# First attention of a gated block: rows turned before they are normalised, the norm applied in the additions, and four engine programs reordered

## The chip, the cores and the metric

One core of one Trainium2 chip runs the whole kernel as one program. The metric is the device time of one execution in microseconds; lower is better.

## The reference

Two layers of gated cross-attention and feed-forward work on x (4 x 256 tokens of 256 features) beside a context of 4 x 256 rows of 128. LN is a layer norm without gains.

```python
# layer 0, attention: the mixing is along the features of x
q = ctx @ Wq0.T + bq ; k = ctx @ Wk0.T + bk           # [4, 256, 128]
att = softmax(q @ k.T, -1)                            # [4, 256, 256], its rows sum to 1
x = x + tanh(g_xattn[0]) * einsum('bln,bmn->blm', LN(x), att)
# layer 0, feed-forward: both products with ternary weights and rows rounded to 8 bits
x = x + tanh(g_ffn[0]) * bit_linear(silu(gate) * up, down_w)    # gate, up = bit_linear(LN(x), gate_w)
# layer 1, attention: 16 heads of 128, q and k with an rms norm
x = x + tanh(g_xattn[1]) * heads(LN(x), ctx, Wq, Wk, Wv) @ Wo
# layer 1, feed-forward: 64 experts, the best 8 of a row, and a shared one
x = x + tanh(g_ffn[1]) * moe(LN(x))
```

With r = 1 / sqrt(var + eps) and m = the mean of a row of x, the first mixing is r * (x @ att.T) - r * m, because every row of att sums to 1. A constant added to a row doesn't change its LN.

## The kernel before

The 1024 tokens are 8 row tiles of 128 (two for each of 4 batches b). Each engine has one program in which the order of the steps is written out by hand as far as the first six of 32 groups of the second attention (a group is one pair of heads of one batch, AHEAD = 6); from there a loop over g runs in the same order for all groups, and then the experts follow. Engines meet through semaphores: a step begins with the waits it needs and ends with an increment. A step that waits holds up everything behind it in its engine's program.

The steps that matter here, by engine:

- SyncE issues all loads in one fixed order: ctxT, the first attention's weights, x in two halves (l_x), the gate weights, gains, down weights, then the head weights `raw` of pairs 0 and 1 (l_hqk, line 326), and more. Its later loads wait for a step: load_vo(2) for fuse_vo(0), load_qk(2) for low_w(0).
- TensorE: query_key (L829) and energy (L844) make the scores of the first attention; turn_rows_0 (L807) turns the normalised rows u of a batch; turn_att (L852) turns its attention, mix (L862) multiplies both. turn_q1, gate_0, up_0 (L878, L885) and turn_q2, down (L904, L912) are the feed-forward, one row tile at a time. fuse_vo (L1026) multiplies value and output weights. turn_rows_1 (L815) turns the normalised rows for the second attention, proj_q and proj_k (through the helper at L310 to L312) are its first products, and scores, turn, values and output its rest. keep_busy is 8 products whose result nobody reads.
- ScalarE: copy_qk (L1472), exp_A (L1478, two instructions with a row sum), copy_rows_0 (L1465), copy_att (L1484), abs_gate and abs_down (L1645, L1652), split_w (L1488: the head weights `raw` rounded into front_hi; it waits for l_hqk), turn_gate (L1506), copy_q1 (L1500), silu_0 (L1514), whole_m (L1596), copy_rows (L1461: the turned rows into xnT_hi).
- VectorE: stats_0 and aggr_0 (L1975, L1980: mean and variance of x), max_A (L2007), inv_A and norm_A (L2011, L2016), add_A (L2025: x + tanh(g) * mix, one instruction for the two tiles of a batch), stats_1, aggr_1, times_g1 and so on for the feed-forward, low_w (L2081: what split_w rounded away), add_down (L2119), low_rows (L1994: what copy_rows rounded away; proj_q(0) waits for it), add_output (the sum of the heads of a batch added to x, in the loop).
- GpSimd: root_0 and power_0 (L476, L477, L482) make -m and r; normalise_0 (L554) makes u = (x - m) * r, one instruction for each tile; round_gate, times_gain and the small scale steps serve the feed-forward.

Of the kernel before, what the change touches and what calls it, by code (L numbers as in the profile page):

```python
# [9 lines left out]
ALU = mybir.AluOpType  # L10
# [3 lines left out]
P = 128  # L14
BATCH, SEQ, HID, CDIM = 4, 256, 256, 128
TOK = BATCH * SEQ
TILES = TOK // P
# [15 lines left out]
EARLY = 5  # L33
# [6 lines left out]
def flamingo_kernel(nc, x_tok, ctx_tok, ctxT, qk0, bias0, gains, gate_wT, down_wT, down_tail,  # L40
                    norm_g1, norm_g2, gqk, head_qk, head_vo, router_w, expert_w, shared_w,
                    shared_down, outT, w_rows):
    with ExitStack() as ctx:
# [35 lines left out]
        rstd = sb("rstd", [P, TILES])  # L79
        u = sb("u", [P, TILES, HID])  # L80
# [84 lines left out]
        g_u0, t_u0, a_x0 = sem("g_u0"), sem("t_u0"), sem("a_x0")  # L165
# [281 lines left out]
        def _(pool):  # L447
# [166 lines left out]
            low_ctxT()  # L614
            root_0(0)
            power_0(0)
            normalise_0(0)
            normalise_0(1)
            root_0(1)
            power_0(1)  # L620
            normalise_0(2)
            normalise_0(3)
            root_0(2)
            power_0(2)
            normalise_0(4)
            normalise_0(5)
            scale_gain(g1, l_g1)
            root_0(3)
            power_0(3)
            round_gate(0)  # L630
            root_1(0)
            round_gate(1)
            power_1(0)
            root_1(1)
            power_1(1)
            scale_back_1(0)
            limit_1(0)
            normalise_0(6)
            scale_back_1(1)
            scale_gain(g2, l_g2)  # L640
            normalise_0(7)
            limit_1(1)
            times_gain(0)
            root_1(2)
            power_1(2)
            times_gain(1)
            root_2(0)
            low_ctx()
            scale_back_1(2)
            power_2(0)  # L650
            limit_1(2)
            times_gain(2)
            rms_k(0)
            root_1(3)
            power_1(3)
            times_gain(3)
            scale_back_2(0)
            scale_back_1(3)
            limit_2(0)
            root_2(1)  # L660
            times_rk(0)
            power_2(1)
            times_gain(4)
            limit_1(3)
            root_3(0)
            power_3(0)
            times_gain(5)
            normalise_1(0)
            normalise_1(1)
            scale_back_2(1)  # L670
            times_gain(6)
            limit_2(1)
            root_2(2)
            times_gain(7)
            power_2(2)
            rms_k(1)
            times_rk(1)
            scale_back_2(2)
            root_2(3)
            power_2(3)  # L680
            limit_2(2)
            rms_k(2)
            times_rk(2)
            scale_back_2(3)
            rms_q(0)
            root_3(1)
            limit_2(3)
            power_3(1)
            rms_k(3)
            pool.wait_ge(t_q2, 8)  # L690
            both_w(EARLY)
            normalise_1(2)
            rms_q(1)
            normalise_1(3)
            times_rk(3)
            low_w(EARLY + 1, 0)
            normalise_att(0, 0)
            normalise_att(0, 1)
            rms_q(2)
            root_3(2)  # L700
            power_3(2)
            normalise_att(1, 0)
            rms_k(4)
            normalise_att(1, 1)
            normalise_1(4)
            normalise_1(5)
            times_rk(4)
            rms_q(3)
            root_3(3)
            low_w(6, 1)  # L710
            low_w(EARLY + 1, 2)
            power_3(3)
            normalise_1(6)
            normalise_1(7)
            normalise_att(2, 0)
            normalise_att(2, 1)
# [2038 lines left out]
```

## Time and profile before

| | us |
|---|---|
| median of 3 runs (615.14 to 615.51) | 615.18 |
| the profiled execution | 616.09 |
| its span, first to last instruction | 614.3 |
| busy: TensorE / weight load | 603.3 / 522.6 |
| busy: VectorE / ScalarE / GpSimd | 477.9 / 422.7 / 236.7 |

TensorE's mean granted clock was 1.000 of full speed. Times inside the span are read from its start. The profiled execution is 0.9 us above the median and 1.8 us longer than its own span.

### The profile page before, as it was taken

What the parts mean: (1) busy time and instruction counts of PE and PEld (TensorE: products, weight loads), DVE (VectorE), ACT (ScalarE), POOL (GpSimd) and SP (SyncE); (2) the same over time, 40 slices, a digit from 0 to 9 for tenths busy, and PEclk for the clock granted to TensorE, in tenths of its full rate; (3) what the DMA queues carried; (4) which work ended last, traced back from release to release, by engine and by line L of the source; (5) the groups of instructions that cost most, each with busy time, mean ns of one, the idle gap of its engine ahead of it and who ended that gap; (6) DMA issues with size and microseconds to landing.
All of it is one profiled execution on the core that took longest, in us unless ns stands there. A gap on an engine that the chain in (4) does not pass through costs nothing.

```text
span 614.3 us, 11619 instructions
## 1 busy us (share of the span) xinstructions
PE 603.3 (98%) x3644; PEld 522.6 (85%) x3644; DVE 477.9 (78%) x1139; ACT 422.7 (69%) x1082; POOL 236.7 (39%) x282
## 2 busy tenths in 40 slices
PE   8979999999999999999999999999999999999997
PEld 6757899999999999999998888888887888887886
DVE  3999988987777787688876787788777676777776
ACT  6999999888888888889897344465444444443442
POOL 5999998576665566656662020000000000000000
PEclk9999999999999999999999999999999999999999
DMA  8513202000000000000030545453856466545640
GB/s 299 196 53 102 95 11 78 2 2 2 2 2 2 1 2 2 1 2 1 11 121 3 170 147 154 129 171 96 216 156 167 116 176 175 156 154 149 195 128 34
DMA packets 33653, 56.47 MB, mean 92 GB/s; under 512 B 12800, under 2 KB 13504, under 8 KB 33600
## 3 DMA queue, kind: packets, MB, share of 16 engines
q1 hardware_dynamic: 33312, 55.82, 30.4%
q8 instruction: 26, 0.43, 0.3%
q14 instruction: 27, 0.22, 0.1%
q10 hardware_dynamic: 288, 0.00, 0.0%
HBM read 53.45 MB, written 1.31 MB: 89 GB/s over the span
## 4 chain that ended last, share of the span: by engine, by line
PE 89%; DVE 5%; ACT 4%; issue 1%; POOL 1%; DVEq 0%; ACTq 0%; POOLq 0%
PE bank L310 25%; PE bank L312 25%; PE bank L311 25%; PE bank L985 4%; PE bank L960 2%; PE bank L952 2%; DVE hs L2088 1%; PE bank L912 1%; PE bank L1026 1%; PE bank L829 1%; DVE attT_lo L2182 1%; PE bank L835 1%; ACT att L1575 1%; ACT w L1478 1%; PE bank L815 1%
## 5 line engine op out<-in xcount | busy, mean ns | idle before, releaser
L1623 ACT ACTIVATE inter_hi<-inter 128x512 fp32r<-128x512 f32 x63 | 39.8, 632 | 140.5 <-DVE inter L2287 140.5
L310 PE MATMUL bank<-xnT_hi,front_hi 128*128 128x512 f32 (+1 forms) x260 | 102.0, 392 | 0.0
L312 PE MATMUL bank<-xnT_hi,front_lo 128*128 128x512 f32 (+1 forms) x260 | 101.7, 391 | 0.0
L311 PE MATMUL bank<-xnT_lo,front_hi 128*128 128x512 f32 (+1 forms) x260 | 101.6, 391 | 0.0
L2291 DVE TENSOR_TENSOR inter_lo<-inter,inter_hi 128x512 fp32r<-128x512 f32 x63 | 43.6, 692 | 37.9 <-ACT inter_hi L1623 37.3
L1575 ACT ACTIVATE att<-bank,shift,rq 128x256 f32<-128x256 f32 x128 | 71.3, 572 | 0.0
L596 POOL TENSOR_TENSOR att<-att,rowinv 128x512 f32<-128x512 f32 x60 | 63.1, 1067 | 11.1 <-DVE rowinv L2187 11.1
L2260 DVE TENSOR_TENSOR prod<-gate_s,bank 128x512 f32<-128x512 f32 x63 | 43.3, 687 | 21.6 <-PE bank L312 19.5
L2170 DVE TENSOR_REDUCE rowmax<-bank 128x2 f32<-128x512 f32 x64 | 43.6, 686 | 20.7 <-PE bank L312 20.4
L311 PEld LDWEIGHTS bank<-xnT_lo,front_hi 128*128 128x128 f32 x260 | 48.9, 188 | 11.3
L312 PEld LDWEIGHTS bank<-xnT_hi,front_lo 128*128 128x128 f32 x260 | 48.8, 188 | 11.3
L310 PEld LDWEIGHTS bank<-xnT_hi,front_hi 128*128 128x128 f32 x260 | 48.8, 188 | 11.1
L578 POOL TENSOR_TENSOR rk<-msq,minus_half 128x4 f32<-128x4 f32 x32 | 32.6, 1020 | 66.4 <-DVE msq L2159 66.4
L310 PE MATMUL bank<-inter_hi,front_hi 128*128 128x512 f32 (+1 forms) x130 | 51.2, 394 | 0.0
L312 PE MATMUL bank<-inter_hi,front_lo 128*128 128x512 f32 (+1 forms) x130 | 51.0, 393 | 0.0
L311 PE MATMUL bank<-inter_lo,front_hi 128*128 128x512 f32 (+1 forms) x130 | 51.0, 392 | 0.0
L2287 DVE TENSOR_TENSOR inter<-prod,w_all 128x512 f32<-128x512 f32 x63 | 43.6, 692 | 3.6 <-DVE prod L2260 1.8
L2182 DVE TENSOR_TENSOR attT_lo<-bank,attT_hi 128x512 fp32r<-128x512 f32 x64 | 43.1, 685 | 3.1 <-ACT attT_hi L1564 3.1
L310 PE MATMUL bank<-m_all,o_hi 128*128 128x256 f32 x128 | 39.0, 305 | 0.2 <-DVE o_lo L2197 0.2
L1619 ACT ACTIVATE gate_s<-bank 128x512 f32<-128x512 f32 x63 | 37.0, 588 | 2.2 <-PE bank L312 2.0
L1564 ACT ACTIVATE attT_hi<-bank 128x512 fp32r<-128x512 f32 x64 | 35.5, 601 | 3.5 <-PE bank L985 3.2
L310 PE MATMUL bank<-kh,qh 128*128 128x256 f32 x128 | 36.4, 284 | 0.1
(273 smaller groups left out, 1811.7 us busy)
## 6 DMA issues: line engine op xcount, KB each, us to landing
w_all<-w_rows SPq DMA_DIRECT2D x128, 128.0 KB, 3.0
raw<-in_expert_w SPq DMA_DIRECT2D x32, 384.0 KB, 3.5
wvo_raw<-in_expert_w SPq DMA_DIRECT2D x16, 384.0 KB, 3.5
e_more<-in_expert_w SPq DMA_DIRECT2D x16, 384.0 KB, 3.6
raw<-in_head_qk SPq DMA_DIRECT2D x8, 384.0 KB, 3.1
wvo_raw<-in_head_vo SPq DMA_DIRECT2D x4, 384.0 KB, 3.8
w_keep<-in_head_vo SPq DMA_DIRECT2D x4, 384.0 KB, 3.3
gate_raw<-in_gate_wT SPq DMA_DIRECT2D x2, 704.0 KB, 9.0
```

Source lines behind the costliest of these rows:

```text
L310: pe.matmul(out, l_hi, r_hi_, start=start, stop=False, skip_group_check=True)
L311: pe.matmul(out, l_hi, r_lo_, start=False, stop=False, skip_group_check=True)
L312: return pe.matmul(out, l_lo, r_hi_, start=False, stop=stop, skip_group_check=True)
L596: pool.tensor_tensor(a, a, rowinv[:, n % 2, h, :].unsqueeze(2).broadcast_to([P, 2, SEQ]), ALU.mult).then_inc(g_att, 1)
L1575: act.activation(att[:, n % 2, h, t, :], bank4(SBK[h])[:, t, :], ACT.Exp, bias=shift[:, n % 2, h, t:t + 1], scale=rq[:, n % 4, t * 2 + h:t ...
L1619: act.activation(gate_s[:, slot, :], bank[GB][:, :], ACT.Silu).then_inc(a_silu, 1)
L1623: act.activation(inter_hi[:, slot, :], inter[:, slot, :], ACT.Copy).then_inc(a_Ihi, 1)
L2170: dve.tensor_reduce(rowmax[:, n % 2, h, :], bank4(SBK[h]), AX.X, ALU.max, negate=True).then_inc(v_max, 1)
L2182: dve.tensor_tensor(attT_lo[:, h, :, :], bank4(TBK[h]), f(attT_hi[:, h, :, :]), ALU.subtract).then_inc(v_Tlo, 1)
L2260: dve.tensor_tensor(prod[:, slot, :], gate_s[:, slot, :], bank[UB][:, :], ALU.mult).then_inc(v_mul1, 1)
L2287: dve.tensor_tensor(inter[:, slot, :], prod[:, slot, :], w_all[:, par, :], ALU.mult).then_inc(v_mul2, 1)
L2291: dve.tensor_tensor(inter_lo[:, slot, :], inter[:, slot, :], f(inter_hi[:, slot, :]), ALU.subtract).then_inc(v_Ilo, 1)
```

## The change

Three parts.

1. turn_rows_0 turns x itself, and waits for the load of x; normalise_0 is gone. power_0 makes two small tiles beside r: tg_rstd = r * tanh(g) and tg_mean = m * tg_rstd. add_A scales the product by tg_rstd of its row, in one instruction for each tile; the part -tg_mean is left out of x there and comes in with add_output of the second attention, also one instruction for each tile. Between the two x is read through LN alone.
2. root_0 no longer makes -m.
3. The written-out orders of TensorE, ScalarE, VectorE and GpSimd up to the loop, or to its end where the loop is the rest, are new, with the waits that the new neighbours need. SyncE's program is unchanged.

```diff
             def root_0(b):
                 c = slice(2 * b, 2 * b + 2)
                 pool.wait_ge(v_pw1, b + 1)
-                pool.tensor_scalar(negm[:, c], mv[:, c, 0], -1.0, 0.0, ALU.mult, ALU.add)
                 pool.tensor_scalar(vare[:, c], mv[:, c, 1], 1.0, EPS, ALU.mult, ALU.add).then_inc(g_va0, 1)
 
             def power_0(b):
                 c = slice(2 * b, 2 * b + 2)
                 pool.wait_ge(g_va0, b + 1)
-                pool.tensor_tensor(rstd[:, c], vare[:, c], minus_half[:, 0:2], ALU.pow).then_inc(g_pw1, 1)
+                link_g(pool, pool.tensor_tensor(rstd[:, c], vare[:, c], minus_half[:, 0:2], ALU.pow))
+                if b == 0:
+                    pool.wait_ge(a_tg, 1)
+                link_g(pool, pool.tensor_scalar(tg_rstd[:, c], rstd[:, c], tg[:, 0:1], 0.0, ALU.mult, ALU.add))
+                pool.tensor_tensor(tg_mean[:, c], mv[:, c, 0], tg_rstd[:, c], ALU.mult).then_inc(g_pw1, 1)
-            def normalise_0(i):
-
-                pool.wait_ge(g_pw1, i // 2 + 1)
-                pool.tensor_scalar(u[:, i, :], x[:, i, :], negm[:, i:i + 1], rstd[:, i:i + 1], ALU.add,
-                                   ALU.mult).then_inc(g_u0, 1)
...
             def turn_rows_0(b, bk):
 
-                pe.wait_ge(g_u0, 2 * b + 2)
+                pe.wait_ge(l_x[b // 2], 16)
                 for k in range(KH):
                     for t in range(2):
                         mm = pe.transpose(bank4(bk)[:, k, t * P:(t + 1) * P],
-                                          u[:, 2 * b + t, k * P:(k + 1) * P], ident[:, :])
+                                          x[:, 2 * b + t, k * P:(k + 1) * P], ident[:, :])
...
             def add_A(b, bk):
                 dve.wait_ge(t_oA, b + 1)
-                if b == 0:
-                    dve.wait_ge(a_tg, 1)
-                xb = x[:, 2 * b:2 * b + 2, :]
-                dve.scalar_tensor_tensor(xb, bank4(bk), tg[:, 0:1], xb, ALU.mult, ALU.add).then_inc(v_xA, 1)
+                dve.wait_ge(g_pw1, b + 1)
+                for t in range(2):
+                    i = 2 * b + t
+                    ins = dve.scalar_tensor_tensor(x[:, i, :], bank4(bk)[:, t, :], tg_rstd[:, i:i + 1], x[:, i, :],
+                                                   ALU.mult, ALU.add)
+                ins.then_inc(v_xA, 1)
...
             def add_output(b):
 
                 dve.wait_ge(t_Y, 16 * b + 16)
-                xb = x[:, 2 * b:2 * b + 2, :]
-                dve.tensor_tensor(xb, bank4(YBK), xb, ALU.add).then_inc(v_Y, 1)
+                for t in range(2):
+                    i = 2 * b + t
+                    ins = dve.scalar_tensor_tensor(x[:, i, :], bank4(YBK)[:, t, :], tg_mean[:, i:i + 1], x[:, i, :],
+                                                   ALU.subtract, ALU.add)
+                ins.then_inc(v_Y, 1)
```

The new orders, as far as the text speaks of them. TensorE, first the old and then the new one:

```python
# before
query_key x5; energy(0, 2); query_key(1, 2, 0); energy(1, 6); energy(2, 0); turn_rows_0(0, 1)
pe.wait_ge(a_eA, 4); turn_att(0, 6); energy(3, 3); mix(0, 1); turn_att(1, 2); turn_rows_0(1, 5)
sum_abs([0, 1], 0); turn_att(2, 4); pe.wait_ge(v_abs, 1); mix(1, 0); sum_abs([2], 5); turn_rows_0(2, 7)
fuse_vo(0, 6); pe.wait_ge(v_xA, 2); keep_busy(0, 8); turn_q1(0, 0); turn_q1(1, 7); gate_0(0); up_0(0); mix(2, 4)
# after
query_key x4; energy(0, 2); query_key x2; turn_rows_0(0, 1); energy(1, 6); energy(2, 0); energy(3, 3)
turn_rows_0(1, 5); pe.wait_ge(a_eA, 4); turn_att(0, 6); mix(0, 1); turn_att(1, 2); turn_att(2, 4)
sum_abs([0, 1], 0); turn_rows_0(2, 7); pe.wait_ge(v_abs, 1); mix(1, 0); sum_abs([2], 5)
pe.wait_ge(v_xA, 2); keep_busy(0, 8); turn_q1(0, 0); mix(2, 4); gate_0(0); turn_q1(1, 7); fuse_vo(0, 6); up_0(0)
```

ScalarE's program up to silu_0(0), as a diff:

```diff
             high_ctxT()
             copy_qk(0, 0, 0, 1)
+            gates()
             copy_qk(1, 0, 1, 7)
             copy_qk(0, 1, 2, 5)
             copy_qk(1, 1, 3, 4)
-            gates()
+            exp_A(0, 2)
             copy_qk(0, 2, 4, 3)
             copy_qk(1, 2, 5, 0)
-            exp_A(0, 2)
+            copy_rows_0(0, 1)
+            split_w(0)
             exp_A(1, 6)
-            copy_rows_0(0, 1)
             exp_A(2, 0)
             copy_att(0, 6)
             abs_gate(0)
...
             copy_att(1, 2)
             copy_rows_0(1, 5)
             abs_down()
-            split_w(0)
-            turn_gate(0)
             exp_A(3, 3)
             copy_att(2, 4)
+            copy_rows_0(2, 7)
+            turn_gate(0)
             turn_gate(1)
-            copy_rows_0(2, 7)
             copy_q1(0, 0)
             load_table(ACT.Silu)
             silu_0(0)
...
             copy_q2(2, 4)
+            act.wait_ge(t_z1, 8)
+            whole_m(3, 6)
             copy_rows(0, 0, 1)
-            whole_m(3, 6)
```

VectorE's program up to the second row tile's sums:

```python
# before
stats_0(0); aggr_0(0); stats_0(1); max_A(0, 2); max_A(1, 6); aggr_0(1); inv_A(0); max_A(2, 0); norm_A(0)
inv_A(1); stats_0(2); aggr_0(2); stats_0(3); norm_A(1); aggr_0(3); inv_A(2); max_A(3, 3); add_A(0, 1)
norm_A(2); weight_scale(0, 0, 2 * INTER * HID); inv_scale(0); stats_1(0); aggr_1(0); times_g1(0)
# after
max_A(0, 2); stats_0(0); aggr_0(0); stats_0(1); inv_A(0); norm_A(0); aggr_0(1); max_A(1, 6); max_A(2, 0)
stats_0(2); aggr_0(2); stats_0(3); max_A(3, 3); inv_A(1); norm_A(1); inv_A(2); norm_A(2); add_A(0, 1)
stats_1(0); weight_scale(0, 0, 2 * INTER * HID); aggr_1(0); inv_scale(0); aggr_0(3); times_g1(0)
```

GpSimd begins with root_0(0), power_0(0), root_0(1), low_ctxT, root_0(2), scale_gain(g1), power_0(1), power_0(2), root_1(0), power_1(0) where low_ctxT stood first and normalise_0 followed each power_0. From there to the loop neighbours change places in all four programs; the set of steps of each engine is the same but for normalise_0.

## Rows read from the trace of the kernel before

**Rows 1.** The page, busy time of each engine.
```profile
PE 603.3 (98%) x3644; PEld 522.6 (85%) x3644; DVE 477.9 (78%) x1139; ACT 422.7 (69%) x1082; POOL 236.7 (39%) x282
```

**Rows 2.** Busy time in chosen stretches; last three columns: TensorE clock, DMA share, GB/s.
```profile
24.50:53.00 28.50, 23.73 (x152) 16.13 (x153) 28.27 (x68) 28.10 (x62) 27.08 (x36) 1.00 0.21 64
55.50:105.00 49.50, 49.50 (x392) 44.99 (x390) 43.63 (x126) 48.22 (x144) 45.72 (x58) 1.00 0.24 81
105.00:115.00 10.00, 9.80 (x78) 9.32 (x77) 8.96 (x30) 8.00 (x27) 6.18 (x6) 1.00 0.01 3
17.33:56.27 38.94, 33.90 (x215) 24.11 (x214) 38.56 (x95) 38.10 (x80) 36.82 (x50) 1.00 0.28 87
```

**Rows 3.** TensorE in order of time.
```profile
13.98 0.63 PE L852 MATMUL bank<-ident,w 128*128 128x128 f32 x4 [0.96 <-DVE invA L2011]
...
15.31 1.98 PE L862 MATMUL bank<-w,xT 128*128 128x256 f32 x8
...
57.18 0.39 PE L310 MATMUL bank<-front_hi,xnT_hi 128*128 128x256 f32 x1
```

**Rows 4.** ScalarE in order of time: start us, length us; idle before it in brackets.
```profile
12.30 0.47 ACT L1478 ACTIVATE w<-bank,nmA 128x256 f32<-128x256 f32 x1
...
13.21 0.59 ACT L1465 ACTIVATE xT<-bank 128x512 f32<-128x512 f32 x1
...
20.28 0.85 ACT L1488 ACTIVATE front_hi<-raw 128x768 fp32r<-128x768 f32 x1
...
27.52 0.83 ACT L1514 ACTIVATE hs<-bank,tinyB 128x704 f32<-128x704 f32 x1
...
49.50 0.69 ACT L1596 ACTIVATE m_whole<-bank,tg 128x512 f32<-128x512 f32 x1 [0.36 <-PE bank L1026]
...
55.49 0.60 ACT L1461 ACTIVATE xnT_hi<-bank 128x512 fp32r<-128x512 f32 x1 [0.43 <-PE bank L815]
```

**Rows 5.** VectorE in order of time.
```profile
17.33 0.75 DVE L2025 SCALAR_TENSOR_TENSOR x<-bank,tg,x 128x512 f32<-128x512 f32 x1 [0.54 <-PE bank L862]
17.99 0.61 DVE L2016 TENSOR_SCALAR w<-w,invA 128x256 f32<-128x256 f32 x2
...
26.02 0.95 DVE L2081 TENSOR_TENSOR front_lo<-raw,front_hi 128x768 fp32r<-128x768 f32 x1
...
34.61 1.54 DVE L2081 TENSOR_TENSOR front_lo<-raw,front_hi 128x768 fp32r<-128x768 f32 x1
...
47.32 0.48 DVE L2119 SCALAR_TENSOR_TENSOR x<-bank,tinyB,x 128x256 f32<-128x256 f32 x1
...
56.27 0.68 DVE L1994 TENSOR_TENSOR xnT_lo<-bank,xnT_hi 128x512 fp32r<-128x512 f32 x1
```

**Rows 6.** Tiles raw (first load) and x, their landings, and the DMA stretch between.
```profile
L326 SPq DMA_DIRECT2D raw<-in_head_qk x1: 576/576/576, 5.7 to 5.7; - x1
DMA to landing us min/median/max: 10.6/10.6/10.6
...
L319 SPq DMA_DIRECT2D x<-in_x_tok x2: 432/432/432, 1.6 to 2.1; - x2
...
  DMA x<-in_x_tok: 8.1, 1
...
DMA to landing us min/median/max: 6.4/6.8/7.2
...
5.70:16.30 10.60, 9.64 (x41) 7.07 (x40) 6.91 (x27) 8.26 (x23) 7.92 (x14) 1.00 1.02 383
```

**Rows 7.** GpSimd: all of line 554 (ns min/median/max), then in order of time.
```profile
L554 POOL TENSOR_SCALAR u<-x,negm,rstd x8: 553/554/2249, 10.6 to 29.4; 128x256 f32<-128x256 f32 x8
...
9.23 0.19 POOL L476 TENSOR_SCALAR negm<-mv 128x2 f32<-128x2 f32 x1 [1.03 <-DVE mv L1980]
9.48 0.19 POOL L477 TENSOR_SCALAR vare<-mv 128x2 f32<-128x2 f32 x1
...
25.98 2.25 POOL L554 TENSOR_SCALAR u<-x,negm,rstd 128x256 f32<-128x256 f32 x1
```

More of the change, by code:

```diff
@@ L626, in _ @@
-            normalise_0(5)
-            scale_gain(g1, l_g1)
+            root_1(0)
+            power_1(0)
+            round_gate(0)
+            round_gate(1)
+            root_1(1)
+            scale_back_1(0)
             root_0(3)
+            limit_1(0)
+            power_1(1)
             power_0(3)
[L630 to L637, printed above, removed]
@@ L683, in _ @@
+            scale_back_2(3)
             times_rk(2)
[L684 to L689, printed above, removed]
             pool.wait_ge(t_q2, 8)
             both_w(EARLY)
+            root_3(1)
+            power_3(1)
+            limit_2(3)
+            normalise_att(0, 0)
+            rms_k(3)
+            normalise_att(0, 1)
+            root_3(2)
+            low_w(EARLY + 1, 0)
+            times_rk(3)
@@ L1102, in _ @@
             turn_q1(0, 0)
-            pe.wait_ge(a_x0, 3)
+            mix(2, 4)
+            gate_0(0)
             turn_q1(1, 7)
-            gate_0(0)
+            fuse_vo(0, 6)
             up_0(0)
-            mix(2, 4)
             gate_0(1)
@@ L1110, in _ @@
             turn_att(3, 7)
-            pe.wait_ge(v_xA, 3)
+            pe.wait_ge(t_y1, 2)
+            pe.wait_ge(a_s1, 2)
+            turn_q1(2, 1)
             turn_rows_0(3, 4)
             proj_k(0, 5, True)
-            pe.wait_ge(a_s1, 2)
-            turn_q1(2, 1)
-            pe.wait_ge(v_h1, 2)
+            gate_0(2)
             turn_q1(3, 3)
-            pe.wait_ge(a_q1, 4)
+            mix(3, 4)
+            gate_0(3)
             up_0(2)
-            gate_0(2)
-            mix(3, 4)
-            pe.wait_ge(v_Mlo, 1)
-            proj_k(1, 6, True)
-            gate_0(3)
+            fuse_vo(1, 7)
             up_0(3)
@@ L1697, in _ @@
             copy_q1(1, 7)
-            split_w(1)
+            high_ctx()
             high_m(0, 6)
@@ L1789, in _ @@
+            split_w(7)
             high_o(1)
[L1790 removed]
+            high_att(2, 0)
             raw_q(6, 6)
[L1792 to L1793 removed]
+            high_att(2, 1)
             high_k(4, 4)
[L1795 removed]
             exps(3, 0)
             exps(3, 1)
+            raw_k(6, 2)
+            square_q(6, 6)
+            copy_rows(3, 3, 7)
             high_q(5, 3)
[L1799 removed]
+            exps(4, 0)
             high_o(2)
[L1801 removed]
@@ L2301, in key_gain @@
                                   ALU.mult).then_inc(v_gk, 1)
+            max_A(0, 2)
             stats_0(0)
@@ L2305, in _ @@
             stats_0(1)
-            max_A(0, 2)
+            inv_A(0)
+            norm_A(0)
+            aggr_0(1)
             max_A(1, 6)
-            aggr_0(1)
-            inv_A(0)
             max_A(2, 0)
-            norm_A(0)
-            inv_A(1)
             stats_0(2)
@@ L2345, in _ @@
             round_down()
+            norm_A(3)
+            add_A(2, 4)
+            times_up_0(0)
             scales_1(1)
-            times_up_0(0)
             round_1(2)
-            add_A(2, 4)
-            round_1(3)
             stats_1(2)
```

582 lines of the change are left out of this document (299 added, 283 removed).

## The prediction, made before the changed kernel ran

> **What bounds the kernel now.** I began with the page's first part: TensorE (PE) is busy for 603.3 us of a span of 614.3 [rows 1]. Such a kernel becomes faster only where PE waits, so the next view is busy time by stretch [rows 2]. From 55.5 to 105 us PE is busy for all 49.50 us, and from 105 to 115 it misses 0.2. From 24.5 to 53 us, however, it is busy for 23.73 of 28.50: 4.8 us of waits. In that same stretch ScalarE (ACT) is busy 28.10 and VectorE (DVE) 28.27 of 28.50 us. The reader is to see two regimes: up to about 56 us ACT and DVE have no free time and PE takes what they give; after it PE has no free time. **The start of the second regime plus a fixed amount of PE work is the time.** Its mark is the first product with the normalised rows, proj_q(0), at 57.18 us [rows 3]; the same PE steps stand ahead of it before and after the change. What sets proj_q(0) is ACT's copy_rows(0) at 55.49 [rows 4] and DVE's low_rows(0) at 56.27 [rows 5].
>
> **The change, part by part. The moved split_w(0).** The largest term is one line of ACT's program. split_w(0) rounds the first head weights: it waits for their load (l_hqk[0]) and then takes 0.85 us, of which 0.1 overlaps the next step as on all rows of ACT [rows 4], so 0.75. It moves from behind abs_down to right behind copy_rows_0(0), ahead of exp_A(1). When is its load there? It is issued at 5.7 us and lands 10.6 us later, at 16.3. That this figure counts from the start of the issue is seen from x: its first half, issued at 1.6, lands after 6.4, and DVE waits for it until 8.1 [rows 6]. The ten us are queueing: the DMA engines are full from 5.7 to 16.3 us, at 383 GB/s [rows 6]. SyncE's program isn't changed, so I let the load land at 16.3 again.
>
> When does ACT reach it? Before, exp_A(1) starts at 12.30, and copy_rows_0(0) takes 0.5 after it [rows 4], now ahead of it: 12.8. The new order asks for the first maximum earlier, so that ACT does exp_A(0) before its last two copies, where it had idled for up to a us: 11.8 to 12.8, and I take 12.3. ACT then stands still for **4.0 us**. Behind that wait on ACT's queue are exp_A(1), exp_A(2) and copy_att(0). For them wait DVE's inv_A(1) and PE's turn_att(0), which waited 0.96 us for this group already [rows 3], then mix(0), add_A(0) and all the rest.
>
> ACT's clock after it: from exp_A(1) at 12.30 to silu_0(0) at 27.52 [rows 4] ACT worked without a gap for 15.2 us; 0.5 (copy_rows_0) and 0.75 (split_w) of it now lie ahead, the other steps are the same: 14.0. So silu_0(0) starts at 16.3 + 0.75 + 14.0 = 31.0, against 27.5: +3.5. From there to copy_rows(0) at 55.49 are 27.97 us with two waits of 0.36 and 0.43 [rows 4], so 27.2 of work; to it comes whole_m(3,6), which stood behind, 0.6 like whole_m(2,4) at 49.50 [rows 4]. copy_rows(0) is then at 31.0 + 27.2 + 0.6 = 58.8: **+3.3**.
>
> DVE's clock: exp_A(1) took 0.9 to the next step [rows 4]. It now ends at 16.3 + 0.75 + 0.9 = 17.9, exp_A(2) at 18.9, copy_att(0) at 19.4; from mix(0) to add_A(0) it was 17.33 - 15.31 = 2.0 [rows 3, 5], so add_A(0) starts at 21.4: +4.1. By then DVE has done norm_A(2) as well, which stood behind add_A(0) (0.6 [rows 5]), and owes an aggregate of 0.1: **+3.6**. From 17.33 to 56.27 DVE is busy for 38.56 of 38.94 us [rows 2], so this shift reaches low_rows(0).
>
> **add_A in two pieces.** One instruction of 128x512 (0.75) becomes two of 128x256. The nearest row is add_down, the same operation on the same shapes, 0.48 [rows 5]; less 0.1 of overlap two cost 0.1 more than one, four times: +0.4 to +0.5, all in DVE's full stretch. **add_output in two pieces**, four times in and behind the loop, costs as much; DVE was busy 8.96 of 10 us even at the head of the loop [rows 2], so it is covered: 0, and +0.5 if that cover were gone.
>
> **normalise_0 leaves GpSimd (POOL).** Eight instructions go, seven of about 0.55 and one of 2.25 [rows 7], 6.1 us, and four negations of 0.25 from start to start [rows 7]. Two tiny ones per batch come, at the same price: 8 x 0.25 = 2.0. POOL gains 5 us. That frees PE's first turn from POOL, but the chain runs over exp_A(1): 0. What DVE gets from it: the same subtraction of DVE (low_w) took 0.95 once and 1.54 another time [rows 5], stretched by 0.6 beside POOL. I take one such stretch less, -0.5, between 0 and three of them, -1.8; it cancels the split of add_A. The turn itself reads x in place of u, same shape: 0.
>
> Here a rule speaks for more. At 25.98 it was POOL's normalise_0 that took 2.25, while DVE's low_w(0) beside it kept to 0.95 [rows 5, 7]. The Trainium skill, SBUF — State Buffer, section "SBUF: two separate sides", has VectorE and GpSimd under an exclusive lock in which the loser blocks fully. By it, had DVE always been the loser, DVE would get 8 x 0.55 = 4.4 us back; the trace shows POOL as the loser at that place, and ACT's shift would stand in any case.
>
> **The order of the rest, up to 115 us.** DVE starts with max_A(0) and so lets x's statistics wait for energy(0), about 1 us, in a stretch in which it will stand before inv_A(1) anyway: 0. SyncE's load_vo(2) waits for fuse_vo(0), which moves behind turn_q1(1) and slips by some 8 us; its user fuse_vo(2) comes six row tiles later: 0. Root, power and scale steps change places on a POOL that has time now: 0. For the remaining shuffles I take 0; the bounds are -2.4 (half of PE's 4.8 us of waits go) and +1.0 (one new wait like the 0.96 of [rows 3]).
>
> **The sum.** proj_q(0) starts when the later of two chains is through: ACT +3.3; DVE +3.6 + 0.5 - 0.5 = +3.6. With some tenths unsure in each I take **+3.4**. Against the profiled execution (616.09 us, span 614.3) that is 619.5; against the median of 615.18, 0.9 under it, **618.6 us**. A measurement of this kernel can tell about 0.2%, 1.2 us, from no change.
>
> **The rivals.**
> 1. *No stall (faster).* If the load is there when ACT comes, split_w(0) fills a gap. exp_A(1) then starts when its maximum is through, about 13.1, behind the turn that PE now does first: 0.8 later than 12.30, with 1.25 us of ACT's work already done: -0.4; the relief of DVE gives -0.5, PE's shorter waits up to -0.8. **613.5 us.** It decides from a landing before about 13 us. Against it: 10.6 us in the trace and full DMA engines. The Trainium skill, DMA: Bandwidth & Descriptors, section "Anatomy of one DMA", fits 2.0 us plus bytes over 436 GB/s to a single DMA; for 384 KB this is an estimate of 2.9 us, a landing at 8.6 and this rival. The trace disagrees for a load behind others. 8%.
> 2. *The stall is largely won back.* PE's steps are regrouped, so its waits could shrink by half: 618.6 - 2.4 = **616.2 us**. For it: proj_k(0), fuse_vo(0) and mix(2) have moved. Against it: ACT and DVE were full, and a full engine makes up no time by order alone. 14%, of which 6 lie within 1.2 us of before.
> 3. *The stall plus a new wait.* DVE sets the end with no relief (+3.6 + 0.5), and one of the many new orders is late by 1.0: **620.3 us**. 13%.
>
> **How the numbers follow.** The forecast has 65%, over 617.4 to 619.7. The range 616.2 to 620.2 takes in most of the second and half of the third rival; outside are the first rival (8), the best of the second (4) and the tail (7). Faster by over 0.2%: 5 of the first rival's 8, 0.05; within: its other 3 and 6 of the second, 0.09; slower: 0.86.
>
> **What would show it.** In the changed profile: ACT idle for about 4 us before front_hi<-raw, released by the DMA of raw; exp_A(1) at 17.0; add_A(0) near 21.4; silu_0(0) near 31.0; proj_q(0) near 60.6; PE full after it; POOL's busy time 4 us less. It is wrong if split_w(0) starts before 14 us, or if proj_q(0) comes before 59 although ACT waited, or if PE shows new waits beyond 60 us.

## The result, and the profile after: 627.1 us, 1.9% slower

The changed kernel takes 627.12 us (median of 4 runs, 626.47 to 627.28), the kernel before 615.35 us beside it (615.14 to 615.74). The ratio is 1.0189, with a 95% interval of 1.0171 to 1.0206. The forecast of 618.6 us had the sign right and the size wrong: +3.4 us were foreseen, +11.8 came, and 627.1 is outside the range of 616.2 to 620.2.

The page of the changed kernel, busy time of each engine and granted clock of TensorE in 40 slices; before stands in [rows 1]:

```profile
span 625.2 us, 11628 instructions
PE 606.5 (97%) x3644; PEld 523.4 (84%) x3644; DVE 481.0 (77%) x1147; ACT 423.4 (68%) x1082; POOL 232.5 (37%) x278
...
PEclk9799999999999999999999999999999999999999
```

The span is 10.9 us longer, but PE is busy only 3.2 us longer, for the same 3644 matmuls; so some 7.7 us are waits, and about 3.2 are matmuls that took longer. (The medians are 11.8 us apart and the spans 10.9, because the profiled execution of the kernel before lies 0.9 us above its median and this one, 627.04, does not.) PEclk says where: the second slice of 15.6 us holds a 7. In the kernel before that line has no such digit. POOL lost 4.2 us of work, as forecast.

ScalarE of the changed kernel in order of time (start, length, what; in brackets the idle time ahead and what ended it), against [rows 4]:

```profile
10.95 0.61 ACT L1482 ACTIVATE xT<-bank 128x512 f32<-128x512 f32 x1
16.19 0.84 ACT L1505 ACTIVATE front_hi<-raw 128x768 fp32r<-128x768 f32 x1 [4.63 <-DMA raw<-in_head_qk]
16.94 0.46 ACT L1495 ACTIVATE w<-bank,nmA 128x256 f32<-128x256 f32 x1
...
24.06 0.60 ACT L1501 ACTIVATE w<-bank 128x512 f32<-128x512 f32 x1 [2.02 <-PE bank L843]
```

The first part of the forecast is there to the tenth: split_w(0) waits for the load, which lands at 16.2 (16.3 was said), and exp_A(1) starts at 16.94 (17.0). The wait itself is 4.63 rather than 4.0, because ACT arrives at 11.6 and not at 12.3. The last row is new: copy_att(1) waits another 2.02 us, and it waits for TensorE.

The chain that ended last goes through the same place (start, length, what):

```profile
5.77 10.39 DMA raw<-in_head_qk
...
16.19 0.84 ACT front_hi L1505
17.03 1.82 ACT w L1495 x8
...
19.39 3.78 PE bank L853 x8
```

TensorE and VectorE there, against [rows 3, 5]:

```profile
12.96 0.60 PE L798 MATMUL bank<-ident,x 128*128 128x128 f32 x4
18.04 0.63 PE L843 MATMUL bank<-ident,w 128*128 128x128 f32 x4 [4.48 <-issue]
19.39 3.78 PE L853 MATMUL bank<-w,xT 128*128 128x256 f32 x8 [0.72 <-ACT w L1501]
22.97 1.92 PE L843 MATMUL bank<-ident,w 128*128 128x128 f32 x8
```

```profile
23.21 0.88 DVE L2044 SCALAR_TENSOR_TENSOR x<-bank,tg_rstd,x 128x256 f32<-128x256 f32 x2 [3.51 <-PE bank L853]
```

The 3.78 us of mix(0) are the surprise. The same eight matmuls took 1.98 before [rows 3]. Busy time in two stretches of this kernel (stretch, length; PE, PEld, DVE, ACT, POOL with counts; granted clock, DMA share, GB/s):

```profile
13.40:18.00 4.60, 0.16 (x2) 0.00 (x0) 1.75 (x7) 1.81 (x6) 3.74 (x9) 1.00 1.04 370
18.00:26.00 8.00, 7.24 (x29) 6.19 (x30) 3.61 (x17) 5.98 (x12) 0.04 (x1) 0.57 0.40 140
```

While ACT waits for the load, PE stands idle; and when PE works again, its granted clock is 0.57 on average over eight us, close to the lower of its two levels (1.2 of 2.4 GHz). The stall is followed by a slow stretch that the forecast did not have. The Trainium skill, TensorE: Matmul & The Clock Gate, section "Part 1: The HAM clock gate", has the clock go back to the lower level on an array that idles; these rows agree.

The mark that closes the first regime, in the three engines:

```profile
63.62 0.63 PE L806 MATMUL bank<-ident,u 128*128 128x128 f32 x4 [0.94 <-POOL u L559]
65.94 0.38 PE L312 MATMUL bank<-front_hi,xnT_hi 128*128 128x256 f32 x1
```

```profile
64.29 0.60 ACT L1478 ACTIVATE xnT_hi<-bank 128x512 fp32r<-128x512 f32 x1 [0.98 <-PE bank L806]
```

```profile
64.92 0.69 DVE L2013 TENSOR_TENSOR xnT_lo<-bank,xnT_hi 128x512 fp32r<-128x512 f32 x1 [1.56 <-ACT xnT_hi L1478]
```

proj_q(0) starts at 65.94, not at 60.6; and all three engines have a wait ahead of it that they did not have before, handed on from POOL's u. Nor is PE full behind it, as the windows show against the 49.50 of 49.50 us in [rows 2]:

```profile
60.00:90.00 30.00, 28.60 (x223) 24.06 (x223) 26.21 (x76) 27.97 (x72) 26.77 (x37) 1.00 0.28 93
90.00:120.00 30.00, 29.00 (x226) 27.02 (x225) 25.52 (x72) 28.04 (x97) 24.82 (x31) 1.00 0.13 41
120.00:150.00 30.00, 29.95 (x230) 28.17 (x230) 26.51 (x76) 24.18 (x76) 18.42 (x18) 1.00 0.01 1
```

Set out by marks (starts in us; the last column is the first operation of the first expert, ScalarE's inter_hi, read from all instructions on that tile):

| kernel | add_A(0) | silu_0(0) | proj_q(0) | first expert |
|---|---|---|---|---|
| before | 17.33 | 27.52 | 57.18 | 336.5 |
| forecast | 21.4 | 31.0 | 60.6 | |
| after | 23.21 | 33.47 | 65.94 | 347.2 |

Up to silu_0(0) the changed kernel loses 5.95 us (3.5 forecast), from there to proj_q(0) another 2.8 (none), and behind proj_q(0) 2.0 (none): 10.7 together.

The marks of before are late, and that explains why 10.7 is not 11.8. Its profiled execution spends 3.78 us on the first ten products (query_key); the kernel with split_w(0) moved alone, which has the same program up to there, spends 2.83:

```profile
5.17 3.78 PE L829 MATMUL bank<-ctxT_raw,wqk 128*128 128x256 f32 x10
```

```profile
5.32 2.83 PE L829 MATMUL bank<-ctxT_raw,wqk 128*128 128x256 f32 x10
```

Its exp_A(0) starts at 11.30, there at 10.49: 0.8 us later before any step that differs. What varied here are the first few products of an execution, so times since the start can be off by this much between two profiles of the same kernel. Distances between two marks of one trace, from silu_0(0) on, are free of it, and they are used below where tenths matter.

### The profile page after: what moved, and what is told of

The parts are those of the page before. It is cut to its first block, busy times and chain, and to the rows that moved or that the text cites. A ratio compares the mean times of both kernels' runs of the same rounds, so it can differ in the third digit from the quotient of the medians.

```text
span 625.2 us, 11628 instructions
## 1 busy us (share of the span) xinstructions
PE 606.5 (97%) x3644; PEld 523.4 (84%) x3644; DVE 481.0 (77%) x1147; ACT 423.4 (68%) x1082; POOL 232.5 (37%) x278
## 3 DMA queue, kind: packets, MB, share of 16 engines
HBM read 53.45 MB, written 1.31 MB: 88 GB/s over the span
## 4 chain that ended last, share of the span: by engine, by line
PE 83%; POOL 6%; DVE 3%; ACT 3%; issue 2%; DMA 2%; SPq 1%; DVEq 0%; ACTq 0%; POOLq 0%
PE bank L312 24%; PE bank L314 24%; PE bank L313 23%; PE bank L976 4%; PE bank L951 2%; PE bank L943 2%; DMA raw<-in_head_qk 2%; POOL w L571 2%; ACT att L1592 1%; DVE k_sq L2175 1%; PE bank L903 1%; PE bank L806 1%; PE bank L853 1%; DVE attT_lo L2203 1%; POOL tinyB L498 1%
## 5 line engine op out<-in xcount | busy, mean ns | idle before, releaser
L595 POOL TENSOR_TENSOR att<-att,rowinv 128x512 f32<-128x512 f32 x60 | 62.9, 1063 | 15.6 <-DVE rowinv L2208 15.5
```

The lines of the kernel that those rows point to most:

```text
L595: pool.tensor_tensor(a, a, rowinv[:, n % 2, h, :].unsqueeze(2).broadcast_to([P, 2, SEQ]), ALU.mult).then_inc(g_att, 1)
```

## The experiments

The first four take the change apart. **split_w(0) alone put back** behind abs_down:

```diff
 copy_rows_0(0, 1)
-split_w(0)
 exp_A(1, 6)
...
 abs_down()
+split_w(0)
```

> The changed kernel with one step of ScalarE's program moved back: split_w(0) stands behind abs_down again. In the changed profile ScalarE waited 4.63 us for the load of raw, TensorE then worked at a granted clock of 0.50 to 0.60 from 19.3 to 26 us, and add_A(0) came at 23.21 against 17.33. Theory A (the stall and what follows from it is the whole loss): no ScalarE wait on a DMA, clock 1.00 throughout, proj_q(0) at 56 to 58 us, time 613.5 to 617. Theory B (the stall and the clock cost about 6 us and the new orders themselves another 5 to 6, through GpSimd's program): add_A(0) near 17.5 again, but proj_q(0) at 60 or later and a time of 619 to 622.

Measured: 620.13 us, ratio 1.0078 (1.0061 to 1.0095), granted clock 1.00, in the range of Theory B, though proj_q(0) came at 59.04 and not at 60 or later. One line of ACT's program is worth 7.0 of the 11.8 us. With it away mix(0) takes 1.99:

```profile
14.68 1.99 PE L853 MATMUL bank<-w,xT 128*128 128x256 f32 x8 [0.69 <-ACT w L1501]
```

But 620.13 is not 615.4: 4.7 us are left, which no stall explains. **The same line moved alone**, in the kernel before:

```diff
 exp_A(0, 2)
+split_w(0)
 exp_A(1, 6)
...
 abs_down()
-split_w(0)
```

> The kernel before with one step moved: split_w(0) stands between exp_A(0) and exp_A(1). All else is the kernel before. ScalarE reaches it at 12.2 and waits until 16.2. Theory A (a stall of 4 us costs, with the half clock it brings on TensorE, 9 to 12 us in any order): 624 to 627. Theory B (it costs its length and the slower clock's 2 to 3 us): 620.5 to 622. My prediction's sum (its length less what ScalarE had waited): 618.5 to 619.5. If TensorE's clock stays at 1.00 here, the half clock needs the longer idle time of the changed kernel.

Measured: 622.15, ratio 1.0107 (1.0090 to 1.0124), +6.7 us, just above Theory B's range and clearly below Theory A's. In the old orders the step costs about as much as in the new ones (6.7 against 7.0), with the same wait and slow products behind it:

```profile
16.08 0.84 ACT L1488 ACTIVATE front_hi<-raw 128x768 fp32r<-128x768 f32 x1 [4.58 <-DMA raw<-in_head_qk]
```

```profile
17.89 1.12 PE L852 MATMUL bank<-ident,w 128*128 128x128 f32 x4 [5.67 <-ACT w L1478]
18.79 1.92 PE L844 MATMUL bank<-w 128*128 128x256 f32 x4
20.50 2.83 PE L862 MATMUL bank<-w,xT 128*128 128x256 f32 x8
```

The first expert starts at 342.3 instead of 336.5, and proj_q(0) at 63.06 instead of 57.18 (5.9 us, and 6.7 with the late start of before): what is lost by proj_q(0) is the whole loss. **The algebra alone**, in all the old orders (x turned by PE, row scalars in add_A and add_output, normalise_0 gone; in the order of before, diff as in part 1 of the change):

> The kernel before with its four orders as they were, and only the first part of the change: TensorE turns x, normalise_0 and the negation are gone, the norm comes in with add_A and add_output, each in two pieces. Both theories: GpSimd's busy time falls by 4 us, VectorE's rises by 1 us; time within 0.5 us of 615.3, as the prediction's sum has it (+0.5 for the pieces, -0.5 for less stretching). If add_A's pieces are felt without relief: 615.8 to 616.3.

Measured: 616.69, ratio 1.0021 (1.0011 to 1.0030). The algebra costs 1.2 us, above both expected ranges; from silu_0(0) to proj_q(0) are 30.7 us where before had 29.7. Against the kernel with split_w(0) back (620.13), the difference is only the order of the steps and the waits that go with it: **the new orders cost 3.4 us**.

**Is it the idle TensorE?** The changed kernel with 16 idle matmuls on a bank that nobody reads, ahead of PE's wait for the exponentials:

```diff
 turn_rows_0(1, 5)
+keep_busy(7, 16)
 pe.wait_ge(a_eA, 4)
```

> The changed kernel with 16 more products of 512 columns that nobody reads, on TensorE ahead of the wait for exp_A(1), so that it is busy during ScalarE's stall of 4.6 us; the stall itself stays. It tells the clock's share from the stall's. If the half clock from 18 to 26 us comes from TensorE's idle time: clock 1.00 throughout, mix(0) takes 1.9 us in place of 3.78, add_A(0) at 21.4 in place of 23.2, and the time falls by 2 to 3.5 us, to 623.6 to 625. If the clock has another cause: no change, 627.1.

Measured: 624.71, ratio 1.0148 (1.0131 to 1.0165); 2.4 us come back though ACT still waits for the load, 4.22 us here. The filler and mix(0) of this kernel:

```profile
13.92 3.93 PE L1010 MATMUL bank<-ctxT_hi 128*128 128x512 f32 x16
...
19.60 1.99 PE L853 MATMUL bank<-w,xT 128*128 128x256 f32 x8 [0.72 <-ACT w L1502]
```

and its windows over the same stretches:

```profile
13.40:18.00 4.60, 4.45 (x22) 3.35 (x20) 2.33 (x8) 1.61 (x5) 4.14 (x8) 1.00 1.03 358
18.00:26.00 8.00, 6.52 (x38) 5.47 (x38) 5.66 (x21) 8.00 (x21) 2.45 (x5) 1.00 0.43 147
```

The clock stays at 1.00, ACT is busy for all 8.00 us where it had 5.98, and silu_0(0) starts at 31.09, add_A(0) at 21.63. Those are the forecast's 31.0 and 21.4: its marks behind the stall were right for a TensorE at full clock. The price in time was not: without the stall silu_0(0) starts at 26.90 (split_w(0) put back), so the stall alone costs 4.2 us at this mark and 4.6 in the medians (624.71 less 620.13), where the forecast had 3.5 at this mark and 3.4 in time. It had subtracted the late 27.52 of before.

**Is the stall a matter of the load's place in the queue?** The changed kernel with SyncE issuing that load right behind x, ahead of the gate weights:

```diff
+sp.dma_start(raw[:, 0, :], head_qk[0]).then_inc(l_hqk[0], 16)
 (gate, down and the other first loads)
-for p in range(2):
+for p in range(1, 2):
```

> The changed kernel (627.1 us) with its four programs untouched; only SyncE issues the first head load, for which ScalarE stood 4.63 us, ahead of the two gate loads, right behind x. If the stall is a matter of the load's landing in its queue: it lands near 10 us, ScalarE doesn't wait, TensorE's clock stays at 1.00, and the time is that of the kernel with split_w(0) moved back, 620.1, less up to 0.5 or, if the gate weights come late for their sums, more by up to 1. If the place of split_w(0) costs by itself (its 0.75 us ahead of exp_A(1)): 620.5 to 621.

Measured: 619.66, ratio 1.0063 (1.0047 to 1.0078). ACT runs into split_w(0) without a wait:

```profile
11.40 0.61 ACT L1483 ACTIVATE xT<-bank 128x512 f32<-128x512 f32 x1
11.87 0.87 ACT L1506 ACTIVATE front_hi<-raw 128x768 fp32r<-128x768 f32 x1
```

The step may stand where the change put it, if its load is issued early: 7.5 us of the 11.8 go. Nothing else of the change was touched, so the wait is the load's and not something of the new neighbours. The gate weights that the load passed cost nothing visible (silu_0(0) at 26.66).

**What does the algebra's 1.2 us consist of?** First, add_A as one instruction (this kernel leaves out the second tile's own scale):

```diff
-for t in range(2):
-    i = 2 * b + t
-    ins = dve.scalar_tensor_tensor(x[:, i, :], bank4(bk)[:, t, :], tg_rstd[:, i:i + 1], ...)
+dve.scalar_tensor_tensor(xb, bank4(bk), tg_rstd[:, 2 * b:2 * b + 1], xb, ALU.mult, ALU.add)
```

> The kernel before with its old orders and the first part of the change (that run took 616.7 us, proj_q(0) at 57.46), but add_A again as one instruction for the two tiles of a batch. It leaves out the second tile's own scale (both use the first tile's), the rest is computed. If the two pieces of add_A are what makes that part slower: VectorE's stretch from add_A(0) to low_rows(0) falls from 39.96 to 39.4 or less and the time by 0.5 to 0.8 us, to 616.0. If it is the order left as it was around steps whose lengths have changed: no change, 616.7.

Measured: 617.15, ratio 1.0016 (1.0007 to 1.0025), against 1.0021 with two: the spans are 614.5 and 614.8, and add_A(0) to low_rows(0) takes 39.86 us, where 39.4 or less was expected against 39.96. The split costs a few tenths at most, and no measurement here parts it from nothing. Then a row of the algebra kernel's VectorE, beside GpSimd's at the same time:

```profile
28.76 0.87 DVE L2022 SCALAR_TENSOR_TENSOR x<-bank,tg_rstd,x 128x256 f32<-128x256 f32 x2
29.55 1.26 DVE L2061 TENSOR_SCALAR w<-w,tinyB 128x256 f32<-128x256 f32 x1
```

```profile
28.97 1.69 POOL L577 TENSOR_TENSOR w<-hs,g 128x704 f32<-128x704 f32 x1
```

round_1(3) takes 1.26 us; the same operation took 0.35 ahead of add_A(2), at 28.50. GpSimd's product began at 28.97 and ended at 30.66, and round_1(3), begun at 29.55, ended at 30.81, just behind it; by these times it made little progress until the product was nearly through. In the kernel with add_A in one piece it is caught just the same (1.31 us from 29.29, the product from 28.75), so the split is not the cause. The trace of before shows what kept them apart: there the product starts at 30.56, behind a normalise_0 of 0.66 at 29.37, and round_1(3), which takes 0.34 from 30.18, is done by then.

```profile
29.37 0.66 POOL L554 TENSOR_SCALAR u<-x,negm,rstd 128x256 f32<-128x256 f32 x1
30.12 0.47 POOL L532 TENSOR_SCALAR tinyB<-tinyB,wsk 128x2 f32<-128x2 f32 x1
30.56 1.70 POOL L572 TENSOR_TENSOR w<-hs,g 128x704 f32<-128x704 f32 x1
```

Without normalise_0 the product starts 1.6 us earlier in the span; half of that is the late start of before. Counted from silu_0(0) it starts 2.2 us behind it instead of 3.0, while round_1(3) begins 2.8 behind it (2.7 before), so that now the two meet. So round_1(3) was put **ahead of add_A(2)**:

```diff
 round_1(2)
-add_A(2, 4)
 round_1(3)
+add_A(2, 4)
```

> The kernel before with its old orders and the first part of the change (616.7 us), with one step of VectorE moved: round_1(3) ahead of add_A(2). In that run round_1(3) took 1.26 us in place of 0.35 and ended 0.15 us after GpSimd's times_gain(0), beside which it ran. If that was the lock of the two engines' shared port: round_1(3) takes 0.35 here, proj_q(0) comes 0.5 to 0.9 us earlier than 57.46, and the time is 615.8 to 616.2. If it was chance, or another instruction is caught in its place: 616.5 to 616.9.

Measured: 615.90, ratio 1.0006 (0.9997 to 1.0015); silu_0(0) to proj_q(0) takes 29.9 us instead of 30.7. The two roundings are one row of 0.61:

```profile
28.59 0.61 DVE L2061 TENSOR_SCALAR w<-w,tinyB 128x256 f32<-128x256 f32 x2
29.11 0.87 DVE L2022 SCALAR_TENSOR_TENSOR x<-bank,tg_rstd,x 128x256 f32<-128x256 f32 x2
```

0.8 us of the 1.2 are this one collision, and the algebra as such costs nothing that can be told from zero. A second collision of the kind stands at 34.20, where VectorE's low_w(1) takes 1.54 instead of 0.95, before the change too [rows 5]. It was taken out as well:

```diff
+low_w(1)
 absmax_1(2)
 absmax_2(0)
 inv_max_1(2)
-low_w(1)
```

> The changed algebra, old orders, round_1(3) ahead of add_A(2) as before, and VectorE's low_w(1) ahead of absmax_1(2), absmax_2(0) and inv_max_1(2): it took 1.54 us at 34.20 beside GpSimd's gain product (33.25, 1.68 us), 0.95 elsewhere. Theory, an operation of VectorE caught by a two-input operation of GpSimd costs its whole stretch when VectorE is busy throughout: low_w back at 0.95, 0.6 us won, 615.3 against 615.9 without this step. Rival: the maximum that now comes 0.9 us later is what ScalarE and TensorE wait for next, and nothing is won, or up to 0.4 lost: 615.9 to 616.3.

```profile
33.20 0.95 DVE L2080 TENSOR_TENSOR front_lo<-raw,front_hi 128x768 fp32r<-128x768 f32 x1
```

Measured: 615.44, ratio 1.0000 (0.9991 to 1.0009). low_w has its 0.95 back. The mark proj_q(0) starts at 56.94, against 56.76 with low_w at 1.54, but this profile began late as well (silu_0(0) at 27.32 against 26.86): from silu_0(0) to proj_q(0) it takes 29.6 us instead of 29.9. The time is near the theory's 615.3, 0.5 us under the kernel without this step, and the intervals of the two ratios overlap. So about half of the 0.6 us may have been won, and these runs don't decide between the theory and its rival. This is the best kernel with the new algebra, and it is the kernel before, to within the measurement.

**Where are the 3.4 us of the new orders?** Marks of the two kernels that differ by the orders alone:

| kernel | silu_0(0) | proj_q(0) | first expert |
|---|---|---|---|
| algebra, old orders | 26.77 | 57.46 | 336.8 |
| algebra, new orders but for split_w(0) | 26.90 | 59.04 | 340.3 |

0.1 up to silu_0(0), 1.5 from there to proj_q(0), 1.9 behind it. Three guesses for it follow. The chain of the second kernel goes through GpSimd ahead of proj_q(0):

```profile
51.30 1.66 POOL w L571
...
53.31 0.94 POOL vare L514
...
55.30 1.29 POOL u L559 x2
```

The first guess was **GpSimd's load**: three gain products at half their columns (they leave out the other half), in the new and in the old orders:

```diff
-pool.tensor_tensor(w2[:, i, :], h_raw[:, i % 2, :], g2[:, :], ALU.mult)
+w = INTER // 2 if i in (2, 3, 4) else INTER
+pool.tensor_tensor(w2[:, i, 0:w], h_raw[:, i % 2, 0:w], g2[:, 0:w], ALU.mult)
```

> The changed kernel with split_w(0) moved back (620.1 us, proj_q(0) at 59.04), and with GpSimd's times_gain of row tiles 2, 3 and 4 over half of the columns: it leaves out the gain of the other half and gives GpSimd 2.5 us back between 34 and 53 us. If GpSimd's full program is what holds this order (the chain runs over it from 31.6 to 56.6 us, and TensorE, ScalarE and VectorE wait for it): proj_q(0) at 57 to 57.8 and a time of 618.2 to 618.9. If VectorE and ScalarE hold it as before: less than 0.5 us.

> The same half of times_gain left out for row tiles 2, 3 and 4, but in the old orders with the first part of the change (616.7 us, proj_q(0) at 57.46). If GpSimd is the holder only in the new order: less than 0.5 us, 616.2 to 616.7. If it is full and binding in both: 1 to 1.5 us less.

Measured: new orders 620.08, ratio 1.0067 (1.0053 to 1.0081), against 620.13; old orders 616.48 against 616.69. The distance from silu_0(0) to proj_q(0), which the start doesn't touch, shrinks by 0.1 us in the new orders (32.14 to 32.06) and by 0.2 in the old ones (30.69 to 30.50). A GpSimd with less to do gives next to nothing back in either: although the chain lies on it, it then stands before VectorE's mean (aggr_2(1)), which comes no earlier: 35.6 us behind add_A(0) with the full products and with the halved ones. The second guess was the **31 waits of PE on its own semaphores** that the new order brought:

```diff
-pe.wait_ge(t_eA, 2)
-pe.wait_ge(t_abs, 1)
-pe.wait_ge(t_oA, 2)
 (and 28 more of the kind)
```

> The changed kernel with split_w(0) moved back (620.1 us), without the 31 waits in TensorE's written-out order for TensorE's own semaphores; each stands ahead of a wait for an engine that itself had to wait for the same value, so nothing is let through that was held. The new order lost 1.9 us between proj_q(0) and the first expert, and shows waits of only 0.8 us more there. If a wait of TensorE for its own work costs the rest (a drain of some 0.05 to 0.1 us each): 618.5 to 619.5. If they are free because the other wait holds it anyway: 620.1.

Measured: 620.32, ratio 1.0072 (1.0058 to 1.0085). They cost nothing that shows: proj_q(0) to the first expert takes 281.3 us instead of 281.2. The third guess was that **the mean comes too late**:

```diff
 add_down(1, 3)
-round_2(2)
 stats_2(1)
-absmax_2(4)
 aggr_2(0)
 aggr_2(1)
+round_2(2)
+absmax_2(4)
 (GpSimd: times_gain(5) from behind limit_1(3) to behind normalise_1(1))
```

> The changed kernel with split_w(0) moved back (620.1 us, proj_q(0) at 59.04, where TensorE, ScalarE and VectorE wait 0.94, 0.97 and 1.55 us for the turned rows of normalise_1), with the steps that lead there moved ahead: VectorE's aggr_2(0) and aggr_2(1) ahead of round_2(2) and absmax_2(4), GpSimd's root_3(0), power_3(0) and normalise_1(0), (1) ahead of times_gain(5). If the order of these few steps is what holds the new order: the waits vanish, proj_q(0) at 57.5 to 58.2, time 618.5 to 619.3. If other work of VectorE and ScalarE is late by as much: less than 0.4 us.

Measured: 622.55, ratio 1.0105 (1.0090 to 1.0121): worse by 2.4. The mean did come 0.85 us earlier (51.42 instead of 52.27), but the gain product that had to make room is what the next row tile stands on. Rows of VectorE, then of TensorE:

```profile
57.02 0.89 DVE L2116 TENSOR_REDUCE amax<-w 128x1 f32<-128x704 f32 x1 [2.11 <-POOL w L571]
```

```profile
59.96 0.61 PE L895 MATMUL bank<-ident,w 128*128 128x128 bf16 x6 [2.57 <-DVE hs L2109]
60.60 0.55 PE L312 MATMUL bank<-front_hi,xnT_hi 128*128 128x256 f32 x1
60.95 0.41 PE L313 MATMUL bank<-front_lo,xnT_hi 128*128 128x256 f32 x1
```

and its window behind that wait:

```profile
60.60:64.00 3.40, 3.40 (x16) 3.40 (x17) 3.40 (x9) 2.16 (x5) 2.47 (x4) 0.52 0.00 0
```

This run shows the other mechanism a second time: TensorE waits 2.57 us, and the products behind it take 0.41 instead of 0.28 at a granted clock of 0.52.

The last try was to **cut the four programs** at one point (ahead of the fourth tile of scores, about 95 us), at which in every program the same steps lie ahead of the cut in both orders. One kernel has the old orders up to it and the new ones behind, the other the reverse. TensorE's program around the cut, old then new:

```diff
 turn_q(4, 7)
 proj_q(6, 6, True)
-scores(3); turn_rows_1(3, 7); turn(2, 0); turn_k(4, 4)
+turn(2, 0); scores(3); turn(2, 1); turn_k(4, 4)
...
```

> The changed algebra with the old orders up to the fourth tile of queries' scores (about 95 us into the span) and the new orders behind it, in all four programs. Old orders throughout took 616.69, new ones throughout 620.13. Theory A, the new orders lose where they differ, by what they run late, and each loss stays: at the fourth scores the new orders stood 2.76 us behind the old (97.54 against 94.78), so only the rest, some 0.7 us, falls behind the cut: 617.4. Rival B, the two halves of the new order belong together (the first half does work early that the second half then needs): the second half alone loses more, 618 to 620. Rival C, the loss up to the cut is given back and the real one sits behind it: 619.5 to 620.

> The mirror image: the new orders up to the same cut, the old ones behind it. Theory A: 616.69 + 2.76 = 619.4, and the first expert's first operation near 339.5. Rival B: as much as both halves together or more, 620 and over. Rival C: 617 or less, since the old second half gives back what the new first half had only moved.

Measured: old then new 621.98, ratio 1.0105 (1.0090 to 1.0121), +5.3 us over the old orders throughout; new then old 633.88, ratio 1.0301 (1.0287 to 1.0315), +17.2. Both are worse than either whole. Of the three, only Rival B fits, and the first kernel lies above its 618 to 620: the losses do not add by place. In the second, TensorE's clock adds its share: from 105.8 to 112 us, behind the wait of 4.54, it is granted 0.75. PE stands behind the cut as the steps of one half wait for what the other half did in another sequence, in the first and in the second kernel:

```profile
97.88 0.63 PE L982 MATMUL bank<-ident,att 128*128 128x128 f32 x4 [1.99 <-ACT k_raw L1556]
101.70 0.63 PE L957 MATMUL bank<-ident,k_raw 128*128 128x128 f32 x4 [1.33 <-DVE o_lo L2212]
```

```profile
105.82 1.09 PE L806 MATMUL bank<-ident,u 128*128 128x128 f32 x4 [4.54 <-POOL u L559]
```

**What stays open.** The 3.4 us are the orders' (the two kernels differ in nothing else but the waits that go with them), and half are lost by proj_q(0), half by about 130 us: the next tiles of scores start 3.45 us apart at 134 us, and stay so. Which of the exchanged neighbours does it was not found; GpSimd's load and the waits on own semaphores are excluded, and the mean's place as far as it was tried.

## Why the prediction was right or wrong

**What bounds the kernel: right.** The loss at proj_q(0) stands in the end time, in all kernels with the old orders behind it: 279.3 to 279.4 us lie between proj_q(0) and the first expert before, with the algebra alone and with split_w(0) moved alone. With the new orders it is 281.2 to 281.3.

**The stall: right in kind, place and length.** ACT idle ahead of front_hi, released by the load of raw, 4.63 us against 4.0; exp_A(1) at 16.94 against 17.0. Rival 1 (no stall) fell: the load issued at 5.77 took 10.39 us, and only when issued ahead of the gate weights was it there in time. The fit that the Trainium skill, DMA: Bandwidth & Descriptors, section "Anatomy of one DMA", gives for a single DMA would have had the load land at 8.6 (an estimate). The page has it for DMAs issued from GpSimd, and SyncE issues this one; no run bears it out for a load behind others.

**Missing from the sum: TensorE's clock.** The forecast read in [rows 3] that PE waited for this very group and let everything shift by the stall alone. It never asked what PE does in those 4.6 us. PE idled, then worked at a granted clock of 0.57, and add_A(0) came at 23.21 instead of 21.4, silu_0(0) at 33.47 instead of 31.0. The filler shows it: 2.4 us, and both marks back at 21.63 and 31.09. The stall together with its clock costs 7.0 us, where the forecast had 3.4 for it: 2.4 for the clock, and 4.6 for the stall alone. Of the 1.2 between 4.6 and 3.4, 0.8 is a baseline error: the marks behind the stall hang on the load's landing, and the forecast compared them with a profile of before whose own start was 0.8 us late.

**"For the remaining shuffles I take 0": the step that failed most.** Its bounds were -2.4 to +1.0; it is +3.4, measured as the difference of two kernels with one order each. The upper bound, one new wait like the 0.96 of [rows 3], was taken from a single place, for a change that reorders four programs from end to end. In the forecast's own terms: from silu_0(0) to copy_rows(0) it expected 27.8 us, and ACT took 30.8 (33.47 to 64.29). And the statement that PE has no free time behind proj_q(0) was true of the order that was there, not of any order: the new one loses 2.0 us in the regime that the forecast called full, so that the last of its three signs of being wrong, new waits of PE beyond 60 us, came true. Which exchanged steps cost the 3.4 us stays open.

**POOL and the split of add_A: small, one sign wrong.** POOL's busy time fell by 4.2 us, as said (4; the forecast's own sum had 5). The relief of DVE (-0.5) did not come; in its place came one new collision of +0.9, made by the relief itself, since a GpSimd that has less to do starts its product earlier, by 0.8 us counted from silu_0(0). The forecast read the rule one way only. The trace of before showed POOL as the one that is stretched at 25.98 [rows 5, 7]; in the algebra kernel it is DVE, 1.26 us instead of 0.35, and moving it ahead of add_A(2) won 0.8. That the operation that starts first keeps the ports for its whole length, and the other waits whichever engine it is on, is what the Trainium skill says (SBUF — State Buffer, section "SBUF: two separate sides"). The case of round_1(3) agrees: the product began at 28.97, round_1(3) at 29.55. The case at 25.98 doesn't decide it: normalise_0, the one that was stretched, began 0.04 us ahead of low_w(0). add_A in two pieces (+0.4 to +0.5) was felt as a few tenths at most; add_output in two pieces (0) was right as far as the first expert: 279.4 us behind proj_q(0) with the algebra alone, 279.3 before.

**The sum again, with what was measured:** forecast +3.4, clock +2.4, silu_0(0) to proj_q(0) +2.9 (32.5 us against 29.6 forecast), behind proj_q(0) +2.0: 10.7, of 10.9 in the span; the late start of before makes up most of the rest to 11.8. **By kernels:** 627.12 less 624.71 is the clock, 2.4; less 620.13 the stall, 4.6; less 616.69 the orders, 3.4; less 615.90 the collision, 0.8; the rest is within the measurement. Rival 3 (stall and a new wait, 620.3) had the right shape, with both of its prices too low. That the forecast's sign was right is no luck, since the stall is real; its size missed two causes of 2.4 and 3.4 us.

## What to carry to other kernels

Ahead of a step that waits for a load, read when the load lands behind the others in its queue, not how large it is; if the step must stand there, issue its load earlier (7.5 us here for moving one issue). When a stall leaves TensorE idle, cost the stretch behind it at its lower clock too, or fill the idle time with matmuls that nobody reads. If a time in the forecast hangs on an event of its own, such as a landing, see first whether the profile that it is compared with started late. An order in which the engines are full behaved here as one piece: both halves joined to the other order cost more than either whole, and a few steps pulled forward cost 2.4 us in one place and won 0.8 in another, so "it is only reordered" is no term of zero but one to bound by several waits, in both regimes.

## What the runs showed of the hardware that was not expected

- After 4.5 us without work TensorE ran at a granted clock of 0.57 on average from 18 to 26 us, so that eight matmuls took 3.78 us instead of 1.99. With split_w(0) moved alone the clock had already fallen during the wait, to 0.50 from 16.0 us on. After a wait of only 2.57 us, in a stretch with other gaps (3.40 us busy of the six from 56 to 62), it stood at 0.52 for the next 3.4 us.
- A VectorE operation of 0.35 us with one input in memory took 1.26 beside a GpSimd product of 1.69 that had begun 0.6 us earlier; in the kernel before, the product began just as it was through and did not touch it.
- Thirty-one waits of TensorE on its own semaphores cost nothing that 4 and 5 runs can tell (620.32 against 620.13 us).
- The first ten products of an execution took 3.78 us in one profile and 2.83 in another, with the same program up to there; from 5.2 to 7.0 us the traces have 4 matmuls in the one and 9 in the other, and the granted clock reads 1.00 in both. Everything behind is 0.8 us later. The cause was not looked for.
